# A two-layer transformer block on one core: one indirect DMA of GpSimd at a time

## The reference

```
sa, ca, ga, sb, cb, gb = (silu(c) @ wmod) split in six; ga, gb pushed to at least 0.25 in size
h = layernorm(x) * (1 + ca) + sa
x = x + ga * attention1(h)           # 16 heads of 8, relative position bias, softmax over all keys
h = layernorm(x) * (1 + cb) + sb
x = x + gb * block2(h)
block2(h): h2 = h + attention2(rmsnorm(h, g1))      # rotary, causal
           y  = h2 + moe(rmsnorm(h2, g2))
moe(t): probs = softmax(t @ w_router); the best 2 of 8 experts per token, weights made to sum to 1
        sum over them of weight * (silu(t @ wg[e]) * (t @ wu[e])) @ wd[e]      # 128 -> 384 -> 128
```

## Time and profile before

| | |
|---|---|
| time, median of 3 runs | 968.88 us (968.59 to 970.19) |
| span of the profiled execution (first to last instruction) | 959.7 us |
| around it, to the median of the runs | 9.2 us (the profile gives no time of its own for the execution) |
| mean granted TensorE clock | 0.966 |
| indirect DMAs | 156 on GpSimd: 64 of token rows, 92 of results |
| stage of attention alone | to about 540 us |
| attention and tiles mixed | 540 to 848 us |
| tiles alone, then the last sums | 848 to 959.7 us |

### The profile page before, as it was taken

The page is one execution under the profiler, slowest core; times in us unless marked ns, Lnnn a source line. Parts: engine busy times, 40 slices in busy tenths (PEclk is TensorE's granted clock), DMA queues, the critical chain, the costliest instruction groups (busy, mean ns, idle before and its releaser), DMA issues.

```text
span 959.7 us, 36375 instructions
## 1 busy us (share of the span) xinstructions
PE 834.5 (87%) x15215; PEld 507.8 (53%) x15215; DVE 633.4 (66%) x1534; ACT 553.3 (58%) x974; POOL 337.6 (35%) x451
## 2 busy tenths in 40 slices
PE   6879989989898988979888899987899789879995
PEld 3334444535444544545444455555555556768793
DVE  2547676975887687557757876567584656737773
ACT  3457657667765756745756566744548355425652
POOL 2442232222332342233324302436123544654452
PEclk9999999999999999979999899989999989989998
DMA  7997200000000000000000100011000111124634
GB/s 178 389 346 270 90 24 9 8 25 20 8 25 14 13 24 15 14 18 9 19 19 14 36 24 14 20 29 44 26 19 19 31 40 40 56 62 124 187 90 126
DMA packets 50191, 60.91 MB, mean 63 GB/s; under 512 B 5872, under 2 KB 36464, under 8 KB 49648
## 3 DMA queue, kind: packets, MB, share of 16 engines
q1 hardware_dynamic: 34768, 27.19, 9.7%
q10 hardware_dynamic: 10272, 21.14, 6.4%
q0 software_dynamic: 4992, 10.27, 3.2%
HBM read 22.92 MB, written 35.65 MB: 61 GB/s over the span
## 4 chain that ended last, share of the span: by engine, by line
PE 49%; DVE 27%; issue 9%; ACT 8%; another core or an unknown queue 3%; POOL 1%; DMA 1%; SPq 0%; POOLq 0%; DVEq 0%; ACTq 0%
DVE row_max L1337 13%; PE ps L928 9%; PE ps L755 5%; PE ps L788 5%; PE ps L1013 4%; PE ps L766 4%; PE ps L811 2%; PE ps L1005 2%; PE ps L802 2%; PE ps L1007 2%; PE ps L1006 2%; ACT probs L1165 2%; PE ps L773 2%; PE ps L794 1%
## 5 line engine op out<-in xcount | busy, mean ns | idle before, releaser
L1337 DVE TENSOR_REDUCE row_max<-ps 128x4 f32<-128x1024 f32 (+1 forms) x256 | 268.1, 1078 | 103.0 <-PE ps L766 42.1
L1165 ACT ACTIVATE probs<-ps 128x1024 f32<-128x1024 f32 x128 | 130.3, 1029 | 78.8 <-PE ps L788 56.3
L755 PE MATMUL ps<-bias_t,ch 64*32 64x512 f16 x2048 | 111.3, 395 | 24.8 <-DVE row_max L1337 10.9
L1653 POOL DMA_INDIRECT eo_rows<-eo_t,to_t x92 | 89.7, 975 | 114.5 <-ACT eo_t L1217 93.3
L1165 ACT ACTIVATE stage<-ps 128x1024 f32<-128x1024 f32 x96 | 96.8, 1026 | 29.7 <-PE ps L794 20.7
L1005 PE MATMUL ps<-xT_t,wgu_hi 128*128 128x256 f16 x276 | 78.0, 283 | 23.8 <-DVE row_max L1337 7.0
L1211 ACT ACTIVATE gate_t<-ps 128x256 f32<-128x256 f32 x138 | 52.6, 387 | 67.2 <-PE ps L1007 47.9
L1600 POOL TENSOR_TENSOR ctx_sb<-ctx_raw,ctx_sb 128x512 f32<-128x512 f32 x32 | 41.1, 1284 | 132.0 <-DVE ctx_sb L1365 131.8
L928 PE MATMUL ps<-probs,v_pad 128*32 128x256 f32 x1024 | 85.5, 400 | 1.8 <-ACT probs L1165 1.8
L1640 POOL DMA_INDIRECT slot_rows<-rows,slots x64 | 63.9, 998 | 57.1 <-DVE slots L1441 43.1
L1491 DVE SCALAR_TENSOR_TENSOR gate_s<-gate_t,ps 128x256 f32<-128x256 f32 x138 | 57.2, 415 | 33.9 <-ACT gate_t L1211 31.4
(11 more groups left out here) (170 smaller groups left out, 1603.3 us busy)
## 6 DMA issues: line engine op xcount, KB each, us to landing
slot_rows<-eo_g ACTq DMA_DIRECT2D x1, 12642.0 KB, 46.9
slot_rows<-eo_g ACTq DMA_DIRECT2D x1, 7998.0 KB, 25.9
x_t<-slot_rows SPq DMA_DIRECT2D x46, 129.0 KB
eo_g<-eo_rows SPq DMA_DIRECT2D x16, 256.0 KB
xT<-in_x SPq DMA_DIRECT2D x16, 128.0 KB, 2.1
kept<-resid SPq DMA_DIRECT2D x16, 128.0 KB, 1.7
resid_b<-kept SPq DMA_DIRECT2D x16, 128.0 KB
out_dram<-outT SPq DMA_DIRECT2D x16, 128.0 KB
```

The costliest lines, as they stand in the source:

```text
L755: eng.matmul(ps[HR * c:HR * (c + 1), two[r], :].rearrange("p (j s) -> p j s", j=2), csth("flip")[half, :], bias_t[half, way, 2 * g:2 * g + ...
L1165: eng.activation(probs[a][:, 2 * (k % 2):2 * (k % 2) + 2, :], both_of("c%d" % a, i, "e%d" % k), ACT.Exp).then_inc(z["exp"], 1)
L1337: ins = eng.tensor_reduce(row_max[a][:, qt, 4 * g:4 * g + 4].rearrange("p (r j) -> p r j", r=2), of_heads, AX.X, ALU.max)
L1653: eng.indirect_dma_start(out=eo_rows, out_offset=bass.IndirectOffsetOnAxis(ap=to_t[:, done % 4, t:t + 1].bitcast(U32), axis=0), in_=eo_t[: ...
```

## The change

Two edits go together. In the plan, a step that is an indirect DMA (`rowwise`) can't be placed before the one placed last has been given 2.6 us (`LANDS`), whether that was a scatter of rows or a half of a tile's results; and `back0` of a tile is listed as coming after `back1` of the tile before. `ROWWISE` is the resulting order of all 156. On the chip, `ring_free` makes GpSimd wait, ahead of each indirect DMA, on the semaphore value by which the one before it in that order has landed. Since the planned times change, the order of all engines' instructions can change with them. No computation, buffer or DMA is added or removed.

```diff
--- before.py
+++ after.py
@@ -109,6 +109,13 @@
 
 BUSY, WINDOW, WARM = 0.6, 3.42, 0.215
 SHORT = {"var": 0.2, "rank": 0.13}
+
+LANDS = 2.6
+
+
+def rowwise(key):
+
+    return next((n for n in ("scatter", "back") if key[2][0:-1] == n), None) if key[0] in ("h", "moe") else None
 
 
 def each(bank):
@@ -261,7 +268,8 @@
                         ONE)
                 last = self.op(key + ("act",), "act", 0.42, [key + ("pe",)] + ([("moe", of[done - 2], "landed")] if done > 1 else []),
                                (), "mine")
-                last = self.op(key + ("back0",), "pool", 1.2, [last, ("moe", KIND["tr"][done], "to")])
+                last = self.op(key + ("back0",), "pool", 1.2, [last, ("moe", KIND["tr"][done], "to")]
+                               + ([("moe", of[done - 1], "back1")] if done else []))
                 last = self.op(key + ("back1",), "pool", 1.2, [last])
                 self.op(key + ("landed",), None, 2.0, [last])
             else:
@@ -302,6 +310,7 @@
         place, bank_of, held, mine = {}, {}, {}, {}
         active = []
         self.warm = 0
+        landed = {"scatter": 0.0, "back": 0.0}
 
         def keep_busy(until):
 
@@ -369,6 +378,8 @@
                         t, bank = min((at[b], -b) for b in at)
                         bank = -bank
                 t = max(t, clock[eng])
+                if rowwise(k):
+                    t = max(t, landed["scatter"], landed["back"])
                 if best is None or (t, line(k)) < best[:2]:
                     best = (t, line(k), k, bank)
             t, _, k, bank = best
@@ -378,6 +389,8 @@
                 keep_busy(t)
                 active.append((t, t + SHORT.get(k[2].split(".")[0], us)))
             place[k] = t
+            if rowwise(k):
+                landed[rowwise(k)] = t + LANDS
             end = t
             if eng is not None:
                 if eng == "pe" and m != mode:
@@ -426,6 +439,9 @@
 
 
 PLACE, BANK_OF, HELD, N_WARM = schedule()
+
+
+ROWWISE = sorted((k for k in PLACE if k[0] != "warm" and rowwise(k)), key=PLACE.get)
 
 
 def due(job, i):
@@ -660,6 +676,21 @@
 
         tiles_before = [sum(N_TILE[:g]) for g in range(len(PARTS))]
         part_of = [max(g for g, (s, e) in enumerate(PARTS) if s <= i) for i in range(B)]
+
+        def landed(key):
+
+            if key[0] == "h":
+                i, q = key[1], int(key[2][-1])
+                return s_rows[i % 2], 64 * (i // 2) + 16 * (q + 1)
+            kind, g, n, c = PIECES[key[1]]
+            done = tiles_before[g] + n
+            return s_eo[done % 2], 32 * (done // 2) + 16 * (int(key[2][-1]) + 1)
+
+        def ring_free(eng, *key):
+
+            at = ROWWISE.index(key)
+            if at:
+                eng.wait_ge(*landed(ROWWISE[at - 1]))
 
         def given_back(holder):
 
@@ -1637,6 +1668,7 @@
                         eng.wait_ge(hand["twice"], 2 * (i + 1))
                         if i == PARTS[part_of[i]][0]:
                             eng.wait_ge(s_blank[part_of[i]], 16)
+                    ring_free(eng, "h", i, "scatter%d" % q)
                     eng.indirect_dma_start(
                         out=slot_rows[part_of[i]], out_offset=bass.IndirectOffsetOnAxis(ap=slots[:, i, q:q + 1], axis=0),
                         in_=rows[:, i % 2, k, t, :].bitcast(F32), in_offset=None).then_inc(s_rows[i % 2], 16)
@@ -1650,6 +1682,7 @@
                         if t == 0:
                             eng.wait_ge(moe["eo"], done + 1)
                             eng.wait_ge(moe["to"], done + 1)
+                        ring_free(eng, "moe", k, "back%d" % t)
                         eng.indirect_dma_start(
                             out=eo_rows, out_offset=bass.IndirectOffsetOnAxis(ap=to_t[:, done % 4, t:t + 1].bitcast(U32), axis=0),
                             in_=eo_t[:, done % 2, t, :], in_offset=None).then_inc(s_eo[done % 2], 16)
```

## The result

The changed kernel takes 998.6 us (median of 4, 998.17 to 1002.1) against 969.5 of the kernel before: a ratio of 1.031 (95% interval 1.029 to 1.034). That is slower by 29 us where I had forecast 7 us faster; it lies inside my range only by 1.4 us, and on the other side. The number is the one that I had given to the rival *the stalls stay*, but the profile shows that this is luck of the number alone: the stalls went.

A forecast was written before the change was run, and what follows sets the result against it. TensorE was taken as the bound, starved during bursts of indirect DMAs and limited by matmul work in the last stage. Span 959.7 - 37 + 30 = 952.7 us, plus 9.2 around it, gave 962 us; range 941 to 1000.

The forecast's parts named there:

- the stalls stay: Rival: every indirect DMA starves TensorE, so spreading gains nothing and the last stage's loss stands alone: 999 us, chance 0.17.
- What a wait costs: Between GpSimd's indirect DMAs: least distance of starts grows from 1.27 to 2.5 us, taken as 2.7 in the last stage.
- Loss of the last stage: GpSimd's two waits a tile become the bound after the last rows' scatter: 124.2 us instead of 94.4, loss 29.8.
- 2 × 2.7 = 5.4 us: Last stage: GpSimd's time for a tile with two waits, more than TensorE's 3.71 us.
- 23 tiles: Last stage: tiles whose 46 scatters follow from 849.99 us on, each taken at 5.4 us.
- Gain by the stall and the clock: TensorE around bursts: 25 us from fewer stalls plus 12 from the clock, 37 together, bounds 19 and 61.
- The wait's cost in the mixed stage: GpSimd work queued behind waiting indirect DMAs: put at 0, since the planner can fill gaps; bounds 0 and 16 us.
- lands no later: Last burst before the first part's end: the planner ranks rows first, so the last row's landing is not delayed.
- both signs: Forecast wrong if the rows' last scatter ends near 845 us, or last-stage tiles take more than 5.8 us.
- The 9.2 us around the span: Outside the span: 9.2 us from the profiled span of 959.7 to the median of 968.9, added to the forecast span.
- GpSimd's chain is longer: Rival: stalls go, but slower landings and two leftover tiles make the last stage 150 us: 987 us, chance 0.2.

The follow-up runs named there:

- the first part at 2.0 us: The changed kernel with its change only up to the last scatter of rows, planned distance 2.0 us instead of 2.6: 959.2 us (0.989) with the stall.
- the fills: The kernel before, no waits added, with an unread GpSimd computation between scatters of one sequence: 935.3 us (long), 932.6 us (short), with the stall.

## Why the prediction was wrong

*What a wait costs.* Right for a second half of a result: 2.49 us from start to start, against 2.5 forecast. A first half takes 3.00. In the burst of the attention stage that stood at 289.06 before, the four scatters start at 284.10, 287.20, 290.09 and 293.38.

*Loss of the last stage*, forecast 29.8 us. The mechanism was right, the size low. From the last sequence's slots to the end of the span it was 124.5 us and is 163.6, a loss of 39 (45.4 without the stall); the kernel with this part alone loses 43, and taking it away from the whole change brings back 44. The mis-sized term is the tile's 2 × 2.7 = 5.4 us. It measured 5.94: the first half starts 0.77 us after the landing that it waits for and not 0.27, which makes the floor 5.49 (I had read the 0.27 us off an instruction whose late wait was another one), and slow transfers add the rest (twelve landings of 2.5 to 4.6 us in the chain between 864 and 951 us, 2.22 or 2.23 each from 951.65 on). The other factor, 23 tiles, was wrong too: 20 were left behind the last scatter of rows, and some 10 us of waiting for the first tile of part 2 stood in the place of the three others (GpSimd idle 8.73 us ahead of 864.23), so that the product came nearer than its factors (from 851.95 us to the last landing at 981.3 it was 129.4 us, against 124.2).

*Gain by the stall and the clock*, forecast 37 us (bounds 19 and 61). Right in mechanism in the condition of the runs: 35 matmuls became 100, and of the time at the lower clock in the attention stage (134 to 540 us) some 31 us became 10, as the granted clocks of 0.96 and 0.99 say. Worth 47 us up to the last slots, by the difference of the two conditions. But I took the stall for a property of the kernel. The trace of one execution could not show that; in three of the five later series there was no stall at all, and there the change costs 92 us of 889.

*The wait's cost in the mixed stage.* **This is the step that failed**: "I put this at 0, with bounds of 0 and 16 bursts × 1 us". It is 45 us. 33 of them come with the new order alone, with no wait on the chip, and 12 with the waits. I had argued that the planner knows the distance and fills the gaps; it does, but its new order computes 17 tiles ahead of sequence 13 where the old one computed 11, and 26 ahead of sequence 16 where the old one computed 21, and the whole last stage hangs on the last sequence. And the sentence that the last row "lands no later" was wrong: it landed 3 us later, behind two halves of results. So both signs that I had named for a wrong forecast came: the rows' last scatter ended at 851 us instead of 810, and a tile of the last stage took more than 5.8 us.

Put together: 45 + 39 - 47 = +37 us of span; forecast were 0 + 30 - 37 = -7. The sum closes by the way it is made, since the 47 are the 45 and the 2 us of the table; what the experiments measured by themselves are the 45 us without the stall, in their parts of 33 and 12, and the price of the last stage.

*The rule of the Trainium skill* (DMA: Bandwidth & Descriptors, section Rules for kernel authors: issue early and wait late) agrees with the runs of the whole change: the same plan is slower with the waits than without them in both conditions, 981.0 us against 925.9 and 998.6 against 986.1 (ratios to the kernel before of 1.103 against 1.041, and 1.031 against 1.020). It doesn't say that every wait loses: with the stall, waits among rows alone won 2.5% and the first part at 2.0 us won 1%. The fixed cost of the page's section on the anatomy of a GpSimd DMA (an estimate of 2.15 us for 64 KB) agreed with the trace once more: 2.22 us at the least from issue to landing in the changed kernel's last stage.

*The 9.2 us around the span* was a wrong constant: the changed kernel's profiled execution took 998.7 us with a span of 996.8, 1.9 us around it, and the later runs of the kernel before show the same (966.51 us with a span of 964.7). So the profiled execution of before took about 961.6 us, 7 less than the median that I set it against.

*The rivals.* The stalls did not stay, though the number agreed. *GpSimd's chain is longer* was nearest: the stalls go, and the chain of landings costs more than they gave; it had 0.2. It had tiles left over from the first part, where the runs showed the opposite, tiles pulled forward, and it missed that 33 us would come from the order.

## What to carry to other kernels

Don't chain a queue's transfers by their landings in a stage that has nothing else to hide them: two landings of 2.2 us a tile became the bound of a stage of 3.8 us a tile, at once and in full. If transfers that follow too closely disturb another engine, set them apart with work of their own engine rather than with a wait, and only those that lie in bursts (here 932.6 and 935.3 us with the fills against 941.9 with waits among the rows, all with the stall). And before you count on a gain from a stall, see that the stall is there at more than one time: one trace can't tell.

## What the runs showed of the hardware

- The same program ran at 890 and at 967 us on the same chip in different series. In the condition with the stall TensorE starts a third of its matmuls while indirect DMAs of GpSimd follow each other at 1.27 us (35 in 3.8 us against 109), and ScalarE and VectorE wait with it (4.06 and 4.50 us). What makes the condition is not settled; no run here varied it on purpose.
- In that condition, starts 1.8 to 1.9 us apart avoid most of the stall although the transfer before hasn't landed. 9 us of it remain even with full waits (slots of sequence 10 at 506.1 against 496.9 without the stall). Between 1.27 and 1.8 us nothing was measured with the stall.
- Three waits ahead of one indirect DMA: with the wait for the landing behind the two others the DMA started 0.77 us after the landing (975.83 to 976.60), with that wait issued first 0.27 us after it. Both chains have a wait in a row of its own on POOLq just ahead of that start (L693 and L1685), so why the order counts is not shown.
- Landings of indirect DMAs in a chain took 2.22 or 2.23 us where little else was moved (from 951.65 us on) and up to 4.64 us in the last stage ahead of that.
